# Local attention with probabilities, q and k transposed in halves of 64 rows, two row halves of TensorE in turn, and new engine orders

## What is computed

```
q, k, v = split(shift_tokens(x) @ Wqkv)          # 16 heads of 64
q = l2norm(q) * qs ; k = l2norm(k) * ksc
q = q*cos*scale + rotate_half(q)*sin*scale       # k with 1/scale
sim = einsum(q, k of this window of 32 and the one before) * 8
out = einsum(softmax(where(mask, -max, sim)), v)
x   = out @ Wo + x
x   = (a * gelu(gate)) @ W2 + b2 + x   # a, gate from layernorm(shift_tokens(x)) @ W1 + b1
```

## Time and profile of the kernel before

| what | value |
| --- | --- |
| median of 3 runs | 2502.47 us |
| the profiled execution, its own time | 2502.4 us |
| its span in the trace | 2500.6 us |
| granted TensorE clock, mean over the span | 0.981 of full speed (1.00 in the windows of 200 us from 700 to 2300 us) |
| instructions | 62914 |

### The profile page before, as it was taken

The page is one execution under the profiler, slowest core; times in us unless marked ns, Lnnn a source line. Parts: engine busy times, 40 slices in busy tenths (PEclk is TensorE's granted clock), DMA queues, the critical chain, the costliest instruction groups (busy, mean ns, idle before and its releaser), DMA issues. The chain is left out here.

```text
span 2500.6 us, 62914 instructions
## 1 busy us (share of the span) xinstructions
PE 2349.2 (94%) x22929; PEld 1582.4 (63%) x22929; DVE 1917.2 (77%) x2967; ACT 1705.9 (68%) x3296; POOL 1552.8 (62%) x1359
## 2 busy tenths in 40 slices
PE   6899789998799999999999999999999999999995
PEld 3555456665366666666666666666666666666663
DVE  4899957777678778778787787787777787787783
ACT  5888644443577777777777777777777777777763
POOL 4777723222566666676676676676676676676661
PEclk8999999999899999999999999999999999999997
DMA  2312110000122222222221221221221222222221
GB/s 74 109 60 69 55 46 1 1 1 1 46 59 63 63 63 56 69 63 51 74 63 51 71 67 50 66 72 50 64 74 51 63 70 55 63 66 59 63 60 39
DMA packets 102906, 140.33 MB, mean 56 GB/s; under 512 B 63040, under 2 KB 63936, under 8 KB 102336
## 3 DMA queue, kind: packets, MB, share of 16 engines
q1 hardware_dynamic: 102848, 139.57, 20.2%
HBM read 56.39 MB, written 1.31 MB: 23 GB/s over the span
## 5 line engine op out<-in xcount | busy, mean ns | idle before, releaser
L1340 POOL TENSOR_TENSOR f_Pr<-f_Pr,f_rden 128x384 f32<-128x384 f32 x384 | 319.1, 831 | 548.0 <-DVE f_rden L1549 548.0
L1744 PE MATMUL f_psA<-f_W,f_xT 128*128 (+1 forms) x1152 | 581.5, 614 | 11.2 <-DVE f_m L1570 3.7
L1570 DVE TENSOR_TENSOR f_m<-f_psA,f_tab 128x1024 f32<-128x1024 f32 x384 | 455.7, 1217 | 80.3 <-ACT f_sq L1438 54.0
L1365 POOL TENSOR_TENSOR f_qkr<-f_qkr,f_rn 128x1024 f32<-128x1024 f32 x192 | 365.6, 1904 | 28.1 <-DVE f_rn L1608 28.0
L1438 ACT ACTIVATE f_sq<-f_psA 128x512 f32<-128x512 f32 x384 | 222.9, 593 | 119.7 <-PE f_psA L1744 108.1
L1536 DVE TENSOR_REDUCE f_mx<-f_psS 128x8 f32<-128x768 f32 x192 | 178.8, 931 | 143.2 <-PE f_psS L1697 143.2
L1744 PEld LDWEIGHTS f_psA<-f_W,f_xT 128*128 128x128 f32 x1152 | 192.6, 190 | 151.4 <-issue 102.0
L1712 PEld LDWEIGHTS f_psP<-ident,f_Pr 128*96 128x96 f32 x1536 | 176.1, 126 | 167.4 <-issue 104.2
L1728 PEld LDWEIGHTS f_psO<-f_PT,f_V 96*64 96x64 f32 x6144 | 210.7, 137 | 103.3 <-issue 103.1
L1728 PE MATMUL f_psO<-f_PT,f_V 96*64 96x64 f32 x6144 | 263.8, 228 | 0.0
L1357 POOL TENSOR_TENSOR f_qkr<-f_m 128x512 f32<-128x512 f32 x192 | 244.6, 1274 | 9.9 <-DVE f_m L1570 9.9
(11 more groups left out here) (163 smaller groups left out, 4463.1 us busy)
## 6 DMA issues: line engine op xcount, KB each, us to landing
f_V<-f_Vt SPq DMA_DIRECT2D x96, 384.0 KB, 4.2
f_V<-f_Vt SPq DMA_DIRECT2D x96, 256.0 KB, 3.6
f_W<-in_f_W SPq DMA_DIRECT2D x48, 344.0 KB, 3.2
m_Cb<-m_BC_rows SPq DMA_DIRECT2D x64, 256.0 KB, 3.1
f_W<-in_f_W SPq DMA_DIRECT2D x48, 296.5 KB, 3.1
f_V<-f_Vt SPq DMA_DIRECT2D x48, 128.0 KB, 4.8
f_xsA<-xall SPq DMA_DIRECT2D x97, 32.0 KB
f_xsA<-xall SPq DMA_DIRECT2D x97, 31.8 KB
```

Of the source, the lines that this page charges most:

```text
L1340: pool.tensor_tensor(pv, pv, rv.unsqueeze(3).broadcast_to([P, 2, 2, KEYS]), ALU.mult).then_inc(Pr_ready[g][j], 1)
L1365: pool.tensor_tensor(qv, qv, rn[:, j * H:(j + 1) * H].unsqueeze(2).broadcast_to([P, H, DH]), ALU.mult).then_inc(qkr_ready[j], 1)
L1570: dve.tensor_tensor(m12[:, j, :, half].rearrange("p m (h d) -> p m h d", d=DH), psA[n % 2][:, :].rearrange("p (h d) -> p h d", d=DH).unsqu ...
L1744: pe.matmul(psA[n % 2][:, :], xT[:, t, :], weights(i, W_QKV + n * 512, 512), start=True, stop=True).then_inc(A_full[n_fill], 1)
```

## The change

It does four things. Each transpose of 128 rows becomes two of 64 rows, the upper and the lower row half of the array in turn, each half into a PSUM bank of its own. All eight heads of a group go in one call: 16 half transposes in `transpose_probs(g)` (banks `psP` and one bank of `psS`), and 16 in `transpose_qk(g)` (banks `psP` and `psA[g]`), q and k of a group together. `qT` and `kT` become one tile `qkT`, and `PT` is kept by half, so that the number and the size of ScalarE's copies stay as they were (four of `PT`, four of `qkT` in a slot). `scale` on GpSimd works on q and k of eight heads, where it worked on q or k of sixteen: the same 1024 elements. The orders of all engines in a slot are new, and so are the waits that go with the banks.

```diff
-        qT = sb("f_qT", [P, 2, CH, P])
-        kT = sb("f_kT", [P, 2, CH, WIN + P])
+        qkT = sb("f_qkT", [P, 2, 2, CH, WIN + P])
...
+        def probs_bank(g, half):
+
+            return psP[:, :] if g == half else psS[:, g, :]
...
+                if "C" in stages:
+                    normalise_probs(wu, 1, 0)
+                    normalise_probs(wu, 1, 1)
                 if "B" in stages:
                     scale(v, q, 1)
                 if "A" in stages:
+                    rotate(u, t, 1)
                     scaled_tables(u + 1, i + t, 1 - t)
                     rotate(u, t, 0)
                 if "B" in stages:
                     normalise_probs(v, 0, 0)
+                    normalise_probs(v, 0, 1)
...
+                def transpose_probs(g, unit):
+
+                    for j in range(2):
+                        pe.wait_ge(Pr_ready[g][j], unit + 1)
+                    pe.wait_ge(S_free[1], unit + 1)
+                    if g == 1:
+                        pe.wait_ge(P_free[0][0], unit + 1)
                     else:
+                        pe.wait_ge(A_free[6], unit + 1)
...
+                    for h in range(8):
+                        for half in range(2):
+                            r = slice(half * HQ, half * HQ + HQ)
+                            ins = pe.transpose(probs_bank(g, half)[0:KEYS, h * HQ:(h + 1) * HQ], Pr[r, g, (h % 2) * 4 + h // 2, :], ident[r, r])
+                            if h == 7:
+                                ins.then_inc(P_full[g][half], 1)
...
-                    for pair in range(2):
-                        for half, n in ((0, 2 * pair), (0, 2 * pair + 1), (1, 2 * pair), (1, 2 * pair + 1)):
...
+                    for h in range(8):
+                        hh_ = 8 * g + h
+                        ins = pe.matmul(psO[(h % 2) * DH:(h % 2) * DH + DH, h // 2, half * HQ:(half + 1) * HQ],
+                                        V96[:, tile, half, hh_ * DH:(hh_ + 1) * DH], PT[:, half, h, :], start=True, stop=True)
...
+                def transpose_qk(g):
+                    pe.wait_ge(qkr_ready[g], v + 1)
+                    if "A" in stages:
+                        pe.wait_ge(A_free[2 + g], u + 1)
...
+                    if g == 0:
+                        at_least(pe, P_free[1][1], v)
+                    else:
+                        pe.wait_ge(A_free[4], v + 1)
...
+                    for n in range(8):
+                        a, c = divmod(n, 4)
+                        col = a * INNER + (4 * g + c) * P
+                        for half in range(2):
+                            r = slice(half * HQ, half * HQ + HQ)
+                            bank = psA[g] if half else psP
+                            ins = pe.transpose(bank[:, n * HQ:(n + 1) * HQ], qkr[r, q, col:col + P], ident[r, r])
+                            if n == 7:
+                                ins.then_inc(A_full[4 + 2 * g + half], 1)
```

More of the change, by code:

```diff
@@ L1440, in evacuate_qk @@
                 def evacuate_qk(n):
+                    g, half = n // 2, n % 2
                     act.wait_ge(A_full[4 + n], v + 1)
[L1442 to L1445, removed]
+                    src = psA[g] if half else psP
+                    a = WIN + half * HQ
+                    act.activation(qkT[:, q, :, 4 * g:4 * g + 4, a:a + HQ], src[:, :].rearrange("p (a c q) -> p a c q", a=2, c=4), ACT.Copy).then_inc(A_free[4 + n], 1)
                 def gate_gelu(c):
@@ L1475, in slot @@
                 if "C" in stages:
[L1476 to L1481, removed]
+                    evacuate_probs(1, 0, wu)
+                if "B" in stages and q == 1:
+                    act.activation(qkT[:, 1, 1, :, 0:WIN], qkT[:, 0, 1, :, P:P + WIN], ACT.Copy).then_inc(kprev_ready, 1)
                 if "B" in stages:
@@ L1522, in _ @@
             dve.memset(xsC[0:1, 0, 64:D], 0.0)
-            dve.memset(kT[:, 0, :, 0:WIN], 0.0)
+            dve.memset(qkT[:, 0, 1, :, 0:WIN], 0.0)
             dve.memset(V96[0:WIN, 0, 0, :], 0.0)
@@ L1621, in slot @@
                     dve.tensor_tensor(tiles_of(i - 2), psD[0][:, T2:2 * T2].rearrange("p (t d) -> p t d", d=D), tiles_of(i - 2), ALU.add).then_inc(x2_done, 2)
+                if "B" in stages:
+                    denominators(v, 1)
                 if "C" in stages:
@@ L1663, in free_bank @@
                         pe.wait_ge(A_free[n - 2], u + 1)
[L1664 to L1669, removed]
                     elif "B" in stages:
-                        pe.wait_ge(A_free[n - 2], v + 1)
+                        pe.wait_ge(A_free[(5, 7)[n - 8]], v + 1)
                     else:
@@ L1696, in scores @@
                                 k0 = half * HQ
-                                ins = pe.matmul(S4[half * HQ:(half + 1) * HQ, par, c, :], qT[r, q, 4 * g + c, k0:k0 + HQ],
-                                                kT[r, q, 4 * g + c, k0:k0 + KEYS], start=False, stop=True, skip_group_check=True)
+                                ins = pe.matmul(S4[half * HQ:(half + 1) * HQ, par, c, :], qkT[r, q, 0, 4 * g + c, WIN + k0:WIN + k0 + HQ],
+                                                qkT[r, q, 1, 4 * g + c, k0:k0 + KEYS], start=False, stop=True, skip_group_check=True)
@@ L1715, in times_v @@
-                def times_v(g, j, unit, tile):
-                    pe.wait_ge(P_free[g][j], unit + 1)
-                    if j == 0 and g == 1:
+                def transpose_probs(g, unit):
+                    for j in range(2):
+                        pe.wait_ge(Pr_ready[g][j], unit + 1)
+                    pe.wait_ge(S_free[1], unit + 1)
+                    if g == 1:
+                        pe.wait_ge(P_free[0][0], unit + 1)
+                    else:
+                        pe.wait_ge(A_free[6], unit + 1)
+                    alone(pe, passed)
+                    for h in range(8):
[4 more added lines that the diff above has]
+                                ins.then_inc(P_full[g][half], 1)
@@ L1719, in times_v @@
+                def times_v(g, half, unit, tile):
+                    pe.wait_ge(P_free[g][half], unit + 1)
+                    if half == 0 and g == 1:
                         pe.wait_ge(O_free[0], unit + 1)
-                    elif j == 0:
+                    elif half == 0:
                         at_least(pe, x1_ready, unit)
                         pe.wait_ge(V96_ready[tile], (i + (1 if tile == 0 and t == 1 else 0)) * (32, 48)[tile])
-                    for pair in range(2):
-                        for half, n in ((0, 2 * pair), (0, 2 * pair + 1), (1, 2 * pair), (1, 2 * pair + 1)):
-                            h = 4 * j + n
-                            hh_ = 8 * g + h
-                            ins = pe.matmul(psO[(h % 2) * DH:(h % 2) * DH + DH, h // 2, half * HQ:(half + 1) * HQ],
-                                            V96[:, tile, half, hh_ * DH:(hh_ + 1) * DH], PT[:, j, n, half * HQ:(half + 1) * HQ], start=True, stop=True)
@@ L1761, in slot @@
                 if "C" in stages:
-                    transpose_probs(0, 1, wu)
+                    times_v(0, 0, wu, t)
+                    times_v(0, 1, wu, t)
                 if "D" in stages:
```

120 lines of the change are left out of this document (46 added, 74 removed).

## The result

The changed kernel takes 2408.01 us (median of 4 runs, 2406.81 to 2409.31) against 2502.38 for the kernel before in the same comparison: a ratio of 0.9622, with a 95% interval of 0.9606 to 0.9639. The forecast was 2389 us in a range of 2338 to 2466. The profiled execution has 2406.81 us of its own and a span of 2405.0.

The account below looks back on a forecast made before the run. TensorE's list of work was taken to bound the kernel: a pass of 37.83 us, -2.6 of work and +0.2 of waits, gives 35.4; 47 x -2.4 = -113 us takes 2502.4 to 2389 us, 8-in-10 range 2338 to 2466.

Parts of the forecast that it names:

- TensorE's list sets the pass, before and after: Decoder loop: TensorE's work sets the pass of 37.83 us before; other engines' work fits within 35.4 after.
- A half costs 0.027 to 0.031: Transposes on TensorE: one 64-row half costs 0.027 to 0.031 us with row halves overlapping, against 0.107 for a whole.
- The doubt taken from the weight loads: Half transposes: the Trainium skill's rule says a load lasts by its columns, so a half costs as much as a whole.
- A call of 0.66, with 0.1 for going in: Each transpose call: 16 halves 0.45 us plus 0.21 for leaving; entering from full-array work 0.1, three times a slot.
- `times_v` at 1.2 a pair: Paired `times_v` groups on TensorE: 1.2 us a pair with ways in and out, 2.4 for both pairs of a slot.
- The wait for hatC before, 0.56: Kernel before: TensorE's one visible wait, for hatC, 0.56 us a pass beside 37.3 us of work.
- The sum on TensorE: Transposes and `times_v`: 5.35 us a slot against 6.7, so -1.3 a slot and -2.6 a pass.
- Waits of 0.8 a pass, +0.2: TensorE's new waits at project 2, hatC, scores(0), `times_v` and slot head: 0.8 us a pass against 0.56, +0.2.
- The number: Whole kernel: pass from 37.83 to 35.4 us, 47 x -2.4 = -113 us, giving 2389 us.
- Rival 2: VectorE's in-order chain becomes the bound: pass 36.2 to 37 us, 2446 us, up to 2464; chance 0.16.
- its sign, waits of over 1 us a pass behind a table product: What would show VectorE as the bound: TensorE waiting over 1 us a pass behind a table product.
- Rival 3: TensorE calls: entering and leaving costs nothing and waits close, -4.2 us a pass, 2305 us; chance 0.07.

Follow-up runs that it names:

- experiment 3: Changed kernel with every half transpose issued twice: 2554.60 us, ratio 1.0210.
- experiment 5: Changed kernel with VectorE's sum of squares taken over 32 of each head's 64 elements: 2405.28 us, ratio 0.9616.
- 6: Changed kernel without ScalarE's two function table loads in the D slot, GELU replaced by a plain copy with bias: 2408.38 us, ratio 0.9622.
- experiment 2: Changed kernel with both halves of each transpose read from the upper 64 rows, so row halves cannot overlap: 2556.02 us, ratio 1.0210.
- experiment 1: Changed kernel with whole transposes of 128 rows put back, orders and banks as changed: 2438.27 us, ratio 0.9746.
- experiment 7: Changed kernel with the first pair of `times_v` pulled apart, projection 2 between its halves: 2483.21 us, ratio 0.9929.
- 8 to 11: Changed kernel with, in order: projection 0 first; hatC later; both; both plus later statistics: 2417.01, 2417.86, 2417.86 and 2490.40 us.
- experiment 4: Changed kernel with all eight upper halves of a call before all eight lower ones, instead of in turn: 2485.02 us, ratio 0.9930.

## Why the prediction was right, and where it was off

- **TensorE's list sets the pass, before and after.** Right: 3.7 us more work gave 3.15 us more time (experiment 3), less work on VectorE or ScalarE gave none (5 and 6).
- **A half costs 0.027 to 0.031.** Right: 0.028 for the probabilities and 0.031 for q and k, and 0.056 and 0.062 without overlap (2). The doubt taken from the weight loads is settled for transposes: a half's load didn't hold it to 0.107.
- **A call of 0.66, with 0.1 for going in.** Nearly right. It measured 0.58 to 0.65, and the way in and out showed in the neighbours: 0.1 more in the group behind the call, and 0.1 more in most of those before it.
- **`times_v` at 1.2 a pair.** Right in sum: a pair takes 1.08, and projections 0 and 1 ahead of it 1.81 in experiment 1 where they took 1.72 ahead of whole transposes in the kernel before.
- **The wait for hatC before, 0.56.** This is what the view of waits leaves; by starts it was 0.87. So the pass before was 36.96 us of work and 0.87 of wait, not 37.3 and 0.56.
- **The sum on TensorE.** It came to -2.6 us a pass. From the pass of 35.75 and its 1.7 us of waits the work after is 34.05, against 36.96: -2.9. So the sum was 0.3 short.
- **Waits of 0.8 a pass, +0.2.** This term was mis-sized: 1.7, or +0.8 against before, both by starts. (The view of waits has 0.56 before and 0.83 after, just what was forecast; it hides as much as it shows.) The places were the right ones: projection 2 behind the first table product with 0.4 twice where 0.1 to 0.3 was expected, scores(0) with 0.2 for 0.1, and the head of the slot with 0.34 and 0.26 inside its range of 0.1 to 0.4.
- **The number.** The 0.6 us that the waits took more and the 0.3 that the work saved more have opposite signs. They leave the pass 0.35 longer than 35.4; 47 of these are 16 of the 19 us by which the forecast was low. That the error came out so small is in part luck.
- **Rival 2, VectorE as the bound**, falls with experiment 5, and its sign, waits of over 1 us a pass behind a table product, did not show: 0.8 by starts. TensorE's wait for a table product is a matter of the order in which projection, square and product follow one another, not of how much VectorE has to do. **Rival 3** falls with the ways in and out of experiment 1 and with the waits above.
- **What the prediction did not separate** is how much comes from the halves and how much from the groupings and orders. It booked the gain at the transposes of both kinds together; added last, the halves bring a third of it (1).

## To carry to other kernels

Transposes that fill half of the array's rows ran two at a time here when the row halves alternated instruction by instruction: halves of 64 columns cost 0.028 to 0.031 us in turn, 0.056 to 0.062 on one row half, and most of the overlap was lost in blocks of eight. The two halves went to different banks; one bank for both was not tried. Count for each run of such instructions one way in and out (0.1 us on each neighbour here), and put runs of one kind together, but look up what each of the merged runs waits for: a grouping that moves a run ahead of its producer costs more than it saves. In a full in-order queue the work between a product and the wait for what depends on it is a cover; moving it away opens the wait (experiment 7), and the four ways tried here to bring the producer forward only moved the wait (8 to 11). Measure waits by starts, before and after alike: the view of waits showed half of them here, and two thirds in the kernel before.

## What was not expected of the hardware

- The group behind a run of half transposes is 0.10 us longer than behind whole ones, though its own instructions are the same: 0.96 against 0.86 us for a projection, 1.89 against 1.79 for the output projection.
- Of blocks of eight halves only three records of each overlap (experiment 4), with 0.28 us between the first start of one block (1505.64) and that of the other (1505.92). Why the second block starts no sooner is open.
- A pair of `times_v` groups, 32 records, takes 1.08 us, 0.034 a record with its way out, and two groups apart 1.23.
- With 64 columns streamed in both, halves with 96 stationary columns are 0.056 us apart on one row half and those with 128 are 0.062 (experiment 2).
